# One-hot a step sooner in two buffers, gated outputs split on ScalarE and VectorE: the expert loop of a Flamingo-style two-layer kernel

## Chip, cores and metric

The kernel runs on one core of a Trainium2 chip (trn2). The metric is the device time of one execution in microseconds (us), the median of several. TensorE (PE) multiplies, ScalarE (ACT) and VectorE (DVE) work element by element, GpSimd (POOL) too, SyncE (SP) issues the DMAs. Each engine takes its own instructions in order and waits on semaphores for the others.

## The reference, cut to what matters

There are 128 sequences of 64 tokens, 128 features each. Layer 0 is a gated cross attention and then an expert-choice mixture of experts; layer 1 is a gated cross attention and a routed feed-forward. The change touches the mixture of layer 0 alone, and one shared constant.

```python
gates, idx = jax.lax.top_k(affinity, CAP)            # per sequence and expert: CAP = 32 tokens
expert_in = jnp.take_along_axis(x[:, None, :, :], idx[..., None], axis=2)
h = jax.nn.gelu(jnp.einsum('becd,edf->becf', expert_in, w1) + b1[None, :, None, :])
expert_out = jnp.einsum('becf,efd->becd', h, w2) + b2[None, :, None, :]
out = out.at[jnp.arange(b)[:, None, None], idx].add(gates[..., None] * expert_out)
```

There are 16 experts, and a hidden size of 512.

## The kernel before

`run_experts` works in steps: 8 groups of GB = 16 sequences, 16 experts each, so 128 steps, each one expert on the 16 x 32 = 512 chosen rows of a group. In the text, step j is a body of the loop (`body(a)`, j = a.j, e = a.e counts 1 to 16 in a group). What belongs to one step is spread over several bodies:

- In body j TensorE multiplies first-layer products of step j+1 (12 matmuls of 512 columns into psH, L237), then scatters step j-2 into the token sums psA (16 matmuls of 64 rows, 64 columns of weights and 128 moving columns, L1694), then makes the second-layer products of step j (12 matmuls into psE, L237). Ahead of them stand two matmuls ("takes", L1629) that gather rows for the next group. Values are kept as a high and a low half in fp16, and a product takes three matmuls.
- ScalarE copies half of a take (L1734), applies GELU to psH in four parts (`ft` 0 to 3, L1746), and after parts 1 and 3 makes the high half of h (L1751, 1024 elements a partition). In every second body it makes the high half xn of the next normalised tile, ahead of part 2 (L1741).
- VectorE's order in a body: the other half of the take (L1791), the gated output of step j-1 (psE times the gates, into `grow` or `vals` by parity, L1830), in even bodies the next tile (L1772), at e == 2 the residual of the group before (L1864, reads psA), then the one-hot `put` of step j-2 (L1839), the low half of h (L1820, first part), in even bodies `sel` (L1786), the second low half (L1820), in even bodies the split of the tile (L1777), then some statistics (L186).
- GpSimd casts the gated output to fp16 into eoT (L1613) and makes the low half (L1615).
- SP sends eoT through a transposing DMA to eoZ (L1586), then loads the gates of step j+1 (L1578) and, in every second body, rows for a tile (L1546).

`put` is the stationary operand of the scatter: put[p, k, n] is 1 where slot p of tile k holds token n (N = 64). It has one buffer, [P, GT, N] with GT = 8, so that the next one waits until psA of the step before has been made (`seeded["A"]`, j-3). psE, eoT and eoZ have one buffer each too, and psA has one: at the start of a group the bias matmuls (L1685) wait for the residual. Before psE of step j, TensorE waits until step j-1 has been gated, and before the scatter of step j-2 for `put` and for the transposed eoZ of it.

Three lines outside the loop serve as price rows below: L1061 loads 32 columns of `L` (fp32) with a step of 16 elements (64 bytes), L1445 loads 32 columns of `idx32` (fp32) one behind the other, and L1170 copies 1024 two-byte values a partition on VectorE. L766 is a ScalarE copy from SBUF to SBUF of the size that eoT's high half has.

Of the kernel before, what the change touches and what calls it, by code (L numbers as in the profile page):

```python
# [14 lines left out]
F16 = mybir.dt.float16  # L15
# [6 lines left out]
P = 128  # L22
# [82 lines left out]
def _build(nc, whole, I, out):  # L105
# [37 lines left out]
    ident16 = sb(whole, "ident16", [P, P], F16)  # L143
    ident32 = sb(whole, "ident32", [P, P], F32)
    token_of_p = sb(whole, "token_of_p", [P, 1], F32)
    iota = sb(whole, "iota", [P, P], F16)
    eps_col = sb(whole, "eps_col", [P, 1], F32)
    zero_col = sb(whole, "zero_col", [P, 1], F32)
    gates = sb(whole, "gates", [P, 4], F32)
# [39 lines left out]
    def constants_gpsimd(e, s):  # L189
        e.memset(ident16[:], 0.0).then_inc(s["id"], 1)  # L190
        e.memset(ident32[:], 0.0).then_inc(s["id"], 1)
        e.wait_ge(s["id"], 2)
        for m in (ident32, ident16):
            e.affine_select(out=m[:], in_=m[:], compare_op=ALU.not_equal, fill=1.0, base=0,
                            pattern=[[-1, P]], channel_multiplier=1).then_inc(s["ident"], 1)
        e.iota(token_of_p[:], [[0, 1]], base=0, channel_multiplier=1,
               allow_small_or_imprecise_dtypes=True).then_inc(s["iota"], 1)
        e.iota(iota[:], [[1, P]], base=0, channel_multiplier=0,
               allow_small_or_imprecise_dtypes=True).then_inc(s["iota"], 1)
        e.wait_ge(s["ident"], 2)  # L200
        e.wait_ge(s["iota"], 2)
# [1247 lines left out]
    def run_experts(tag, gate, ew, idx16, vals, tok_slot, rows_odd):  # L1449
# [15 lines left out]
        with ExitStack() as c:  # L1465
            weigh = sb(c, "weigh", [P, GB // 4, P], F16)
            xnf = sb(c, "xnfe", [P, 2, D], F32)
            xn = sb(c, "xne", [P, 2, 2, D], F16)
            pick = sb(c, "pick", [P, 2, P], F16)
            EARLY = GT + 1  # L1470
            first_tiles = first_tiles_in(rows_odd)
            sel = sb(c, "sel", [P, 2, NE * CAP], F16)
# [1 line left out]
                  rows_odd]  # L1474
            g32 = sb(c, "g32", [P, FT, ROWS], F32)
            h = sb(c, "h", [P, 2, 2, FT, ROWS], F16)
            put = sb(c, "put", [P, GT, N], F16)
            lnt = sel[:].rearrange("p a k -> p (a k)").bitcast(F32)[:, 0:4 * NT].rearrange("p (k t) -> p k t", t=NT)

            grow = [sb(c, "grow", [P, GB, CAP], F32), vals]  # L1480
            eoT = sb(c, "eoT", [P, GB, 2, CAP], F16)
            eoZ = sb(c, "eoZ", [P, GT, D], F16)
            psH = ps(c, "psH", [P, 4, 512], F32)
# [55 lines left out]
            with nc.Block() as block:  # L1539
# [63 lines left out]
                    all_steps(e, body)  # L1603
                    e.wait_ge(s["next"], 64)

                @block.gpsimd
                def _(e):
                    for n in range(NE * NG):
                        j = flat(0, 0, n)
                        exact = grow[n % 2][:]  # L1610
                        wait(e, s["gated"], j)
                        wait(e, s["turned"], j - 1, 16)
                        e.tensor_copy(eoT[:, :, 0, :], exact).then_inc(s["eo_hi"], 1)  # L1613
                        wait(e, s["eo_hi"], j)
                        e.tensor_tensor(eoT[:, :, 1, :], exact, eoT[:, :, 0, :], ALU.subtract)\  # L1615
                         .then_inc(s["eo_lo"], 1)

                @block.tensor
                def _(e):
                    def batch_rows(par):  # L1620
# [27 lines left out]
                    def body(a):  # L1648
                        j, par = a.j, a.par
                        tpar = a.k % 2  # L1650
                        if a.has_tile(0):
                            if a.bp == 0:
                                wait(e, s["sel"], a.t)
                                wait(e, late["x_hi"], a.t)
                            else:
                                wait(e, late["x_lo"], a.t)
                                wait(e, s["g_0"], a.t, 2, -1)
                            wait(e, s["gelu"], j, FT)
                            take(tpar, a.bp, (psR[:], psH[:, 3, :]))
                        if a.has(1):  # L1660
                            if a.e % NE == NE - 1:
                                t = a.t - 1
                                wait(e, s["g_0"], t, 2)
                                wait(e, s["g_1"], t, 2)
                            for ft in range(FT):
                                wait(e, s["gelu"], j, FT, ft + 1 - FT)
                                if ft == 3:
                                    if a.has_tile(0):
                                        wait(e, s["g_1"], a.t, 2, a.bp - 1)
                                    else:  # L1670
                                        wait(e, s["g_1"], Step(None, 0, NT - 1), 2)
                                last = matmul3(e, psH[:, ft, :],
                                               [w1[:, hl, a.expert(1), ft * P:ft * P + P] for hl in range(2)],
                                               [a.rows(hl, 1) for hl in range(2)])
                                last.then_inc(s["H"], 1)
                        if a.has(-2):
                            wait(e, s["put"], j - 2)
                            wait(e, s["turned"], j - 2, 16)
                            if a.e == 2:
                                wait(e, seeded["xadd"], flat(a.G, 1, -1))  # L1680
                                wait(e, s["weigh"], flat(a.G, 1, 0), 96)
                                for r in range(RT):
                                    for bp in range(2):
                                        rows = slice(64 * bp, 64 * bp + 3 * NE)
                                        last = e.matmul(psA[:, bp, r, :], weigh[rows, r, :], b2[rows], start=r == 0, stop=False, skip_group_check=True)  # L1685
                                last.then_inc(s["bias"], 1)

                            for r in range(RT):
                                for turn in range(2):
                                    for bp in range(2):  # L1690
                                        side = (bp + turn) % 2
                                        rows = slice(64 * bp, 64 * bp + 64)
                                        to = slice(64 * side, 64 * side + 64)
                                        last = e.matmul(psA[to, bp, r, :], put[rows, RT * side + r, :],  # L1694
                                                        eoZ[rows, RT * side + r, :], start=False,
                                                        stop=a.expert(-2) == NE - 1, skip_group_check=True)
                            last.then_inc(s["A"], 1)
                        if a.has(0):
                            wait(e, s["h_lo"], j, 2)
                            wait(e, s["gated"], j - 1)  # L1700
                            for ft in range(FT):
                                last = matmul3(e, psE[:],
                                               [w2[:, hl, a.expert(0), ft, :] for hl in range(2)],
                                               [h[:, par, hl, ft, :] for hl in range(2)],
                                               ft == 0, ft == FT - 1)
                            last.then_inc(s["E"], 1)
# [3 lines left out]
                def _(e):  # L1710
# [18 lines left out]
                    def body(a):  # L1729
# [6 lines left out]
                        for ft in range(FT):  # L1736
                            if ft == 2 and a.bp == 1 and a.has_tile(1):
                                tpar = (a.k + 1) % 2
                                wait(e, late["ln"], a.t + 1)
                                wait(e, s["g"], a.t - 1, 2)  # L1740
                                e.activation(xn[:, tpar, 0], xnf[:, tpar], ACT.Copy).then_inc(s["x_hi"], 1)  # L1741
                            if a.has(1):
                                wait(e, s["H"], j + 1, FT, ft + 1 - FT)
                                if ft % 2 == 0:
# [18 lines left out]
                def _(e):  # L1763
# [48 lines left out]
                    def body(a):  # L1812
# [20 lines left out]
                            queue_tile(a.t + 1, (a.k + 1) % 2)  # L1833
                        if a.e == 2 and a.G > 0:
                            residual(a.G, -1)
                        if a.has(-2):
                            wait(e, seeded["A"], j - 3)
                            of_step = tok_slot[:, a.expert(-2), a.group(-2) * GT:a.group(-2) * GT + GT]
                            e.tensor_tensor(put[:], iota[:, 0:N].unsqueeze(1).broadcast_to([P, GT, N]),  # L1839
                                            of_step.unsqueeze(2).broadcast_to([P, GT, N]), ALU.is_equal)\  # L1840
                             .then_inc(s["put"], 1)
                        h_low(0)
                        if next_tile:
                            select(a.t + 1, (a.k + 1) % 2, False)
                        h_low(1)
                        if next_tile:
                            split_tile(a.t + 1, (a.k + 1) % 2)
                        if a.G == NG - 1 and 4 <= a.e < 4 + 2 * NORM_STAGES and a.e % 2 == 0:
                            stage = (a.e - 4) // 2
                            queue_norm(e, s, lnt, 0, ready1, stage)  # L1850
# [482 lines left out]
```

## Time and profile before

| | |
|---|---|
| median of 3 runs | 1935.6 us (1933.84 to 1941.17) |
| the profiled execution | 1941.25 us, its span 1939.4 us |
| mean granted TensorE clock | 0.974 of full speed |
| PE, DVE, ACT, POOL busy over the span | 93%, 84%, 77%, 49% |
| the expert loop | from about 484 to 1315 us of the span |

The span runs from the first to the last instruction. A busy PE here is not PE at its peak, since matmuls overlap and their ends are modelled; so the distance from one instruction to the same one a step later says more than busy time. A bracket behind an instruction gives the idle time of its engine just before it and who ended it.

### The profile page before, as it was taken

The page shows a single profiled execution, that of the slowest core. Times are in us where ns is not written, and L with a number is a line of the kernel's source. Part 1 is how long each engine was busy: PE and PEld are TensorE (multiplying, and loading weights), DVE is VectorE, ACT ScalarE, POOL GpSimd, SP SyncE. Part 2 cuts the span into 40 slices and gives each one's busy share as a digit, 9 for nine tenths or more (in the row PEclk, how much of TensorE's full clock was granted, in tenths as well). Part 3 has the DMA queues.
Part 4 walks back from the last instruction along what each step waited for, and adds up shares of the span by engine and source line. Part 5 has one row for each costly group of instructions (what it writes and reads, how often), then busy time and mean ns, then how long its engine had stood idle before and what let it go on. Part 6 is the DMA issues. An engine that isn't in the chain of part 4 may idle for free. (4 is left out here: it accounts for less than half of the span.)

```text
span 1939.4 us, 63284 instructions
## 1 busy us (share of the span) xinstructions
PE 1800.5 (93%) x23899; PEld 1080.2 (56%) x23899; DVE 1622.7 (84%) x3128; ACT 1497.9 (77%) x2645; POOL 948.1 (49%) x1174
## 2 busy tenths in 40 slices
PE   6999998895999999999999999887999999999798
PEld 4777786542443334343433434335777777777577
DVE  5999987597888888888888888667999999988754
ACT  5999996575887878787888888665888888888543
POOL 3888886231333333333343333344666666655565
PEclk8999998997999999999999999998999999999899
DMA  7745445495334434443434533534776666644233
GB/s 175 137 95 100 98 93 111 149 362 169 88 90 95 92 89 96 88 98 88 100 88 98 97 91 91 121 83 97 154 161 154 147 148 155 145 83 68 68 110 120
DMA packets 468694, 227.47 MB, mean 117 GB/s; under 512 B 375950, under 2 KB 435254, under 8 KB 468150
## 3 DMA queue, kind: packets, MB, share of 16 engines
q1 hardware_dynamic: 468054, 225.35, 49.6%
q8 instruction: 93, 1.52, 0.3%
q14 instruction: 67, 0.55, 0.1%
q10 hardware_dynamic: 480, 0.05, 0.0%
HBM read 95.88 MB, written 37.09 MB: 69 GB/s over the span
## 5 line engine op out<-in xcount | busy, mean ns | idle before, releaser
L1820 DVE TENSOR_TENSOR h<-g,h 128x1024 f16<-128x1024 f32 x256 | 384.4, 1501 | 121.3 <-ACT h L1751 116.4
L1746 ACT ACTIVATE g<-psH,eb1T 128x512 f32<-128x512 f32 x512 | 330.6, 681 | 44.7 <-PE psH L237 40.7
L237 PE MATMUL psE<-h,ew 128*128 128x512 f16 x1536 | 360.7, 385 | 0.2 <-DVE grow L1830 0.2
L812 POOL TENSOR_TENSOR Ph<-E,Ph 128x512 f16<-128x512 f32 x192 | 222.2, 1157 | 235.8 <-ACT Ph L766 235.8
L1751 ACT ACTIVATE h<-g 128x1024 f16<-128x1024 f32 x256 | 270.5, 1057 | 8.2
L718 ACT ACTIVATE vB<-psV 128x512 f16<-128x512 f32 x384 | 226.1, 589 | 54.4 <-PE psV L616 52.4
L839 DVE TENSOR_TENSOR vB<-psV,vB 128x512 f16<-128x512 f32 x384 | 248.4, 678 | 1.1 <-ACT vB L718 1.0
L237 PEld LDWEIGHTS psE<-h,ew 128*128 128x128 f16 x1536 | 141.5, 99 | 168.7 <-issue 9.8
L616 PE MATMUL psV<-shared 96*64 96x512 f16 x1536 | 210.2, 380 | 1.5 <-DVE vB L839 1.5
L1613 POOL CAST eoT<-grow 128x512 f16<-128x512 f32 x64 | 58.4, 913 | 311.4 <-DVE grow L1830 246.5
L818 POOL TENSOR_TENSOR E<-E,rden 128x512 f32<-128x512 f32 x192 | 200.0, 1042 | 16.3 <-DVE rden L850 15.4
L237 PE MATMUL psH<-shared,ew 128*128 128x512 f16 x768 | 178.2, 382 | 0.0
L237 PE MATMUL psH<-xg,ew 128*128 128x512 f16 x768 | 176.7, 380 | 0.0
L671 PE MATMUL psY<-vB,PT 128*64 128x128 f16 x4608 | 163.6, 220 | 7.9 <-DMA PT<-Ph 6.8
L858 DVE TENSOR_REDUCE top<-psS 128x8 f32<-128x512 f32 x192 | 131.8, 687 | 39.9 <-PE psS L695 39.0
L1613 POOL CAST eoT<-vals 128x512 f16<-128x512 f32 x64 | 43.9, 687 | 245.5 <-DVE vals L1830 197.3
L671 PEld LDWEIGHTS psY<-vB,PT 128*64 128x64 f16 x4608 | 143.7, 110 | 23.9 <-DMA PT<-Ph 15.6
L756 ACT ACTIVATE E<-E,zero_col 128x512 f32<-128x512 f32 x192 | 137.9, 718 | 17.9 <-DVE E L861 15.1
L861 DVE TENSOR_TENSOR E<-psS,top 128x512 f32<-128x512 f32 x192 | 132.8, 692 | 7.8
L695 PE MATMUL psS<-shared,xTa 128*64 128x256 f32 x1024 | 134.4, 383 | 1.9 <-DVE E L861 1.9
L848 DVE TENSOR_REDUCE den<-E 128x8 f32<-128x512 f32 x192 | 130.2, 678 | 5.3 <-ACT E L756 4.3
L627 PEld LDWEIGHTS psU<-shared 96*64 96x64 f16 x3648 | 113.4, 112 | 15.0
(307 smaller groups left out, 3420.0 us busy)
## 6 DMA issues: line engine op xcount, KB each, us to landing
keys_ahead<-shared SPq DMA_DIRECT2D x52, 512.0 KB, 4.7
shared<-keys_ahead SPq DMA_DIRECT2D x52, 512.0 KB, 3.6
grow<-gate_rows SPq DMA_DIRECT2D x64, 256.0 KB, 3.6
vals<-gate_rows SPq DMA_DIRECT2D x64, 256.0 KB
rawe<-in_L_ffn_w_dram SPq DMA_DIRECT2D x32, 256.0 KB, 3.1
wb<-rw SPq DMA_DIRECT2D x64, 128.0 KB, 2.0
idx<-places SPq DMA_DIRECT2D x110, 64.0 KB, 3.0
out_dram<-x SPq DMA_DIRECT2D x7, 512.0 KB, 3.2
```

The source lines that it names most:

```text
L237: last = e.matmul(to, a, b, start=start and n == 0, stop=stop and n == 2, **flags)
L616: last = e.matmul(a.values(b)[half(hp)], cT[:, a.ring, cl, half(b)], Bw[:, bl, a.g, hp].rearrange("p k d -> p (k d)"), start=n == 0, stop= ...
L671: last = e.matmul(psY[half(b), 0:D], PT[:, a4.par, pl, pair, half(b)], vB[:, a4.par, vl, b, pair, :], start=a4.g == n == pair == 0, stop=a ...
L695: last = e.matmul(psS[half(b), h:h + 4, :], xT[:, a.tp, half(b)], u[:, a.slot, h:h + 4, half(b)], start=True, stop=True)
L718: e.activation(vB[:, a.par, 0, b].rearrange("p k d -> p (k d)"), a.values(b), ACT.Copy).then_inc(s["vh" + name], 1)
L756: e.activation(E[:, a1.four], E[:, a1.four], ACT.Exp, bias=zero_col[:], scale=DH ** -0.5)\
L812: e.tensor_tensor(Ph[:, a2.par, 1].rearrange("p k t -> p (k t)"), E[:, a2.four].rearrange("p h l -> p (h l)"), Ph[:, a2.par, 0].rearrange( ...
L818: e.tensor_tensor(E[:, a1.four], E[:, a1.four], rden[:, a1.par, :].unsqueeze(2).broadcast_to([P, 8, N]), ALU.mult)\
L839: e.tensor_tensor(vB[:, a.par, 1, b].rearrange("p k d -> p (k d)"), a.values(b), vB[:, a.par, 0, b].rearrange("p k d -> p (k d)"), ALU.sub ...
L1746: e.activation(g32[:, ft, :], psH[:, ft, :], ACT.Gelu_apprx_tanh, bias=b1T[:, a.expert(1) * FT + ft:a.expert(1) * FT + ft + 1]).then_inc(s ...
L1751: e.activation(h[:, 1 - par, 0, ft - 1:ft + 1, :], g32[:, ft - 1:ft + 1, :], ACT.Copy).then_inc(s["h_hi"], 1)
L1820: e.tensor_tensor(h[:, 1 - par, 1, 2 * q:2 * q + 2, :], g32[:, 2 * q:2 * q + 2, :], h[:, 1 - par, 0, 2 * q:2 * q + 2, :], ALU.subtract)\
```

## The change

`put` gets two buffers and another order of its elements, [P, 2, N, GT]: tokens outermost, the 8 tiles innermost. It is made one body sooner (for step j-1 in body j) and at another place: behind the second low half of h and the tile's split, ahead of the statistics. The constant `iota` grows to [P, N, 8], each token number eight times, so that each operand of the compare is read along its innermost dimension in steps of one element. The scatter's stationary operand is then read with a step of 8 elements (16 bytes). GpSimd has no work in the loop any more: ScalarE makes the high half of the gated output, ahead of GELU part 2, VectorE the low half between the two low halves of h. `pick`, used at the start, lies in the first bytes of `grow[0]`.

```diff
-    iota = sb(whole, "iota", [P, P], F16)
+    iota = sb(whole, "iota", [P, N, 8], F16)
...
-            put = sb(c, "put", [P, GT, N], F16)
+            put = sb(c, "put", [P, 2, N, GT], F16)
...
+            pick = grow[0][:].rearrange("p b c -> p (b c)").bitcast(F16)[:, 0:2 * P].rearrange("p (k t) -> p k t", k=2)
...
-                @block.gpsimd
-                def _(e):
-                    for n in range(NE * NG):
-                        j = flat(0, 0, n)
-                        exact = grow[n % 2][:]
-                        wait(e, s["gated"], j)
-                        wait(e, s["turned"], j - 1, 16)
-                        e.tensor_copy(eoT[:, :, 0, :], exact).then_inc(s["eo_hi"], 1)
-                        wait(e, s["eo_hi"], j)
-                        e.tensor_tensor(eoT[:, :, 1, :], exact, eoT[:, :, 0, :], ALU.subtract)\
-                         .then_inc(s["eo_lo"], 1)
...
-                                        last = e.matmul(psA[to, bp, r, :], put[rows, RT * side + r, :],
+                                        last = e.matmul(psA[to, bp, r, :], put[rows, par, :, RT * side + r],
...
+                            if ft == 2 and a.has(-1):
+                                wait(e, s["gated"], j - 1)
+                                wait(e, s["turned"], j - 2, 16)
+                                e.activation(eoT[:, :, 0, :], grow[1 - par][:], ACT.Copy).then_inc(s["eo_hi"], 1)
...
-                        if a.has(-2):
-                            wait(e, seeded["A"], j - 3)
-                            of_step = tok_slot[:, a.expert(-2), a.group(-2) * GT:a.group(-2) * GT + GT]
-                            e.tensor_tensor(put[:], iota[:, 0:N].unsqueeze(1).broadcast_to([P, GT, N]),
-                                            of_step.unsqueeze(2).broadcast_to([P, GT, N]), ALU.is_equal)\
-                             .then_inc(s["put"], 1)
                         h_low(0)
+                        if a.has(-1):
+                            wait(e, s["eo_hi"], j - 1)
+                            e.tensor_tensor(eoT[:, :, 1, :], grow[1 - par][:], eoT[:, :, 0, :], ALU.subtract)\
+                             .then_inc(s["eo_lo"], 1)
                         if next_tile:
                             select(a.t + 1, (a.k + 1) % 2, False)
                         h_low(1)
                         if next_tile:
                             split_tile(a.t + 1, (a.k + 1) % 2)
+                        if a.has(-1):
+                            wait(e, seeded["A"], j - 3)
+                            of_step = tok_slot[:, a.expert(-1), a.group(-1) * GT:a.group(-1) * GT + GT]
+                            e.tensor_tensor(put[:, 1 - par], iota[:], of_step.unsqueeze(1).broadcast_to([P, N, GT]),
+                                            ALU.is_equal).then_inc(s["put"], 1)
```

## Rows read from the trace of the kernel before

**Rows 1.** Waits in 500 to 1310 us: waiter, releaser: total us, times, longest.

```profile
PE psA L1694 <- DVE put L1839: 27.8, 51, 3.0
PE psA L1685 <- DVE put L1839: 11.2, 7, 1.7
PE psA L1694 <- DMA eoZ<-eoT: 5.7, 8, 4.1
```

**Rows 2.** Busy time by engine in the loop's stretch.

```profile
493.76:1315.00 821.24, 769.62 (x5342) 322.81 (x5340) 681.69 (x867) 653.33 (x916) 281.54 (x254) 0.99 0.42 94
```

**Rows 3.** Timeline of an odd and an even body: start, length, engine, line, idle before.

```profile
839.73 0.42 PE L1694 MATMUL psA<-eoZ,put 64*64 64x128 f16 x16
...
843.10 2.76 PE L237 MATMUL psH<-xg,ew 128*128 128x512 f16 x12
843.21 0.60 ACT L1734 ACTIVATE shared<-psH 128x512 f16<-128x512 f32 x1 [0.65 <-PE psH L1629]
...
843.96 1.33 ACT L1746 ACTIVATE g<-psH,eb1T 128x512 f32<-128x512 f32 x2 [0.15 <-PE psH L237]
...
846.34 0.42 PE L1694 MATMUL psA<-eoZ,put 64*64 64x128 f16 x16 [0.48 <-DVE put L1839]
846.41 1.97 DVE L1820 TENSOR_TENSOR h<-g,h 128x1024 f16<-128x1024 f32 x1
...
846.69 2.76 PE L237 MATMUL psE<-h,ew 128*128 128x512 f16 x12
...
847.77 1.06 ACT L1751 ACTIVATE h<-g 128x1024 f16<-128x1024 f32 x1
...
848.86 1.23 DVE L1820 TENSOR_TENSOR h<-g,h 128x1024 f16<-128x1024 f32 x1 [0.20 <-ACT h L1751]
...
849.71 2.76 PE L237 MATMUL psH<-xg,ew 128*128 128x512 f16 x12
849.82 0.60 ACT L1734 ACTIVATE shared<-psH 128x512 f16<-128x512 f32 x1 [1.00 <-PE psH L1629]
850.00 0.28 DVE L1777 TENSOR_TENSOR xne<-xnfe,xne 128x128 f16<-128x128 f32 x1
850.20 0.29 DVE L186 BATCH_NORM_STATS2 stats<-x 128x6 f32<-128x128 f32 x1
850.40 0.68 DVE L1791 CAST shared<-psR 128x512 f16<-128x512 f32 x1
...
851.00 0.68 DVE L1830 TENSOR_TENSOR grow<-psE,grow 128x512 f32<-128x512 f32 x1
851.59 0.68 DVE L1839 TENSOR_TENSOR put<-iota,tok_slot 128x512 f16<-128x512 f16 x1
...
852.41 0.42 PE L1694 MATMUL psA<-eoZ,put 64*64 64x128 f16 x16
...
```

**Rows 4.** Timeline at the start of a group, body e == 2.

```profile
908.56 1.41 DVE L1864 SCALAR_TENSOR_TENSOR x<-psA,tanh_g,x 128x512 f32<-128x512 f32 x2
...
909.88 1.02 DVE L1839 TENSOR_TENSOR put<-iota,tok_slot 128x512 f16<-128x512 f16 x1
...
910.95 0.40 PE L1685 MATMUL psA<-eb,weigh 48*128 48x128 f16 x8 [1.72 <-DVE put L1839]
```

**Rows 5.** Costliest lines by form: busy us, mean ns.

```profile
L766 ACT ACTIVATE Ph<-E 128x512 f16<-128x512 f32 x192 | 119.1, 621 | 0.6 <-POOL E L818 0.6
L1170 DVE COPY xg<-psXs 128x1024 f16<-128x1024 f16 x16 | 11.0, 687 | 17.3 <-PE psXs L1072 17.3
```

**Rows 6.** Weight loads of three lines, from each line's own view: min/median/max ns.

```profile
L1061 PEld LDWEIGHTS psZ<-ident,L x128: 127/134/149, 357.9 to 374.4; 64*32 64x32 f32 x128
...
L1445 PEld LDWEIGHTS psI<-ident,idx x128: 106/109/171, 443.5 to 456.0; 128*32 128x32 f32 x128
...
L1694 PEld LDWEIGHTS psA<-eoZ,put x2048: 102/107/174, 497.0 to 1313.0; 64*64 64x64 f16 x187
```

**Rows 7.** The view of tile eoZ: its DMA from issue to landing.

```profile
DMA to landing us min/median/max: 3.0/3.1/9.1
```

More of the change, by code:

```diff
@@ L197, in constants_gpsimd @@
                allow_small_or_imprecise_dtypes=True).then_inc(s["iota"], 1)
-        e.iota(iota[:], [[1, P]], base=0, channel_multiplier=0,
+        e.iota(iota[:], [[1, N], [0, 8]], base=0, channel_multiplier=0,
                allow_small_or_imprecise_dtypes=True).then_inc(s["iota"], 1)
@@ L1468, in run_experts @@
             xn = sb(c, "xne", [P, 2, 2, D], F16)
-            pick = sb(c, "pick", [P, 2, P], F16)
             EARLY = GT + 1
```

## Prediction

> **What bounds the kernel now.** I read the page first, for the loop's place, then the busy times of its stretch, the list of waits, the timeline of two bodies, the timeline at a group's start, and last the lines whose shapes price what is new. In the loop TensorE shows 770 of 821 us busy and nearly the full clock (0.99), VectorE 682, ScalarE 653, GpSimd 282 [rows 2]. So TensorE sets the pace where it can, and the question is what it waits for. The list of waits answers: the scatter's matmuls stood 27.8 us, 51 times, until `put` was made, the bias matmuls at a group's start 11.2 us, 7 times, and only 5.7 us were owed to the transposed eoZ [rows 1].
>
> The timeline shows where. From one scatter to the next it is 846.34 - 839.73 = 6.61 us, then 852.41 - 846.34 = 6.07 [rows 3]. The second is TensorE's own work without a gap: 12 matmuls, scatter, 12 matmuls, takes. The first has 0.48 us of idle before the scatter, and is 0.55 longer, as every even body is: there the tile's instruction stands ahead of `put` on VectorE. The reader is to see two more things. ScalarE stands idle before its half of the take, 0.65 us in one body and 1.00 (plus what TensorE was late) in the other [rows 3]: that is its slack. And VectorE's second low half of 1024 elements takes 1.23 us in its quiet moments, but the first 1.97, while GpSimd works too [rows 3].
>
> **Edit 1, `put` a step sooner, in two buffers.** It takes the wait for `put` away in all but the group's first scatter. The waits are 27.8 us of idle, and since 0.48 us of idle stood for 0.55 us of a step, I count 27.8 x 0.55 / 0.48 = 32 us. The new `put` comes at the end of body j for body j+1's scatter, some 1.5 us before it is due (851.1 against 852.4 in the walk below, less what TensorE is held), so nothing of that wait should be left.
>
> **Edit 2, its price on VectorE.** `put` now costs 0.68 us for 512 elements [rows 3]. L1170 moves 1024 two-byte elements in 687 ns [rows 5], the same time for twice the elements, and the new order gives the compare operands that also run in steps of one. From 512 to 1024 fp32 elements VectorE's time grows from 0.68 to 1.23 us [rows 3], so 256 cycles less are about 0.27: I take 0.41 us. The bounds are 0.41 and 0.68.
>
> By the Trainium skill, VectorE: DVE Perf Modes, the perf-mode tier table, a `tensor_tensor` on 16-bit SBUF operands runs at two elements a cycle when all step by one; no such instruction is in this trace, and the row nearest to it, L1170, agrees in rate.
>
> **Edit 3, the strided weights.** Stationary columns now lie 16 bytes apart. The nearest rows: a load of 32 fp32 columns takes 109 ns in sequence and 134 ns with a step of 64 bytes [rows 6], 25 ns more, 0.8 ns a column. A scatter load has 64 columns, so 50 ns more on its 107. The 16 matmuls of 216 ns take 0.42 us together [rows 3, 6], which means four rounds of four quadrants, each round (0.42 - 0.216) / 3 = 0.07 us behind the one before. If the four loads of a round still run side by side, each round is 0.05 longer: 4 x 0.05 = 0.20 us a step, on the path, because TensorE has nothing between. The low end is 0 (two-byte elements and 16 bytes may be read for nothing; L1061 has 64). The high end is that left and right loads, which read the same partitions, take turns: a round is then 2 x (0.07 + 0.05) = 0.24 against 0.07, or 0.67 us a step. I take 0.20, since L1061 is the only strided load there is, and it did pay. Over 127 scatters: 0, +25 or +85 us.
>
> The Trainium skill, SBUF — State Buffer, section on Door 1 (the note on cachelines), speaks against this change: lines are 16 bytes, an operand needs two hits in a line for the full rate, and each access that crosses to a new line pays. L1061 agrees that crossing costs; the page gives no price, and in the same note it calls a step of 8 two-byte elements free, by which the sum would have 0 here.
>
> **Edit 4, eoT on ScalarE and VectorE.** A ScalarE copy of this shape lasts 621 ns [rows 5]; consecutive instructions overlap by 0.08 (VectorE's do: 850.00 + 0.28 against 850.20 [rows 3]), so 0.53 us more in each body, behind the first high half of h. The slack of 0.65 and 1.00 covers it, so ScalarE delays no take; without the slack it would be 0.53 a step. The second high half, and the low half that waits for it, come 0.53 later. VectorE pays 0.68 more for eoT's low half, the time of L1830 in the same size, and gets back what GpSimd cost it (1.97 - 1.23 = 0.74 in that one instruction [rows 3]). It lies between the two low halves, where VectorE would wait for ScalarE.
>
> What is late next is the gating, on which psE waits. Walk the end of an even body: second high half done at 847.77 + 1.06 + 0.53 = 849.36; low half to 850.60; split to 850.80; `put` to 851.13; statistics to 851.34; take copy to 851.94; gating to 852.54. Without any stall, psE would be due 6.06 after 846.69 - 0.55, at 852.20 [rows 3]. So gating is 0.35 late in even bodies, some 50 times: 17 us, if weights cost nothing. With 0.20 in each of the two scatters that lie between (0.40), psE is due at 852.60 and nothing is late. The two costs exclude each other for the most part. In odd bodies there is no tile, split or statistics, and gating is in time.
>
> **The transposes.** They are issued when VectorE's low half of eoT is done: psH's start + 0.86 + 1.33 (two GELUs) + 1.06 (high half) + 1.23 + 0.68, about 5.2 after it, and land 3.1 later [rows 7] at 8.3, while the next scatter is due at 2.69 + 6.06 = 8.75 (the unstalled scatter comes 846.34 - 0.55 - 843.10 = 2.69 after psH's start [rows 3]). Slack 0.45, less than now. Most land in 3.1; a few are slow, and each will cost more: +1.5 us in all.
>
> **The group's start.** There the residual (1.41 us) and `put` (1.02) stand ahead of the bias matmuls, which wait 1.72 [rows 4]. The residual stays, `put` goes, but the body begins about 0.85 later (0.53 from ScalarE, 0.33 for the new `put` of the body before). Residual done at 908.56 + 1.41 + 0.85 = 910.82, against 910.95 now: 0.1 gained, and the stride of one scatter hides in the stall. 7 x 0.3 = 2 us. The stall of 11 us stays: the change does not reach it.
>
> **Sum.** -32 + 25 - 2 + 1.5 = -7.5 us, in the profiled execution 1941.3 (span 1939.4) to about 1934. That execution lies 5.6 above the median, so for the median 1935.6 - 7.5 = 1928, and I say 1928.
>
> **Rivals.**
>
> *Strided loads are free* (0.22). Then -32 + 17 - 1 + 1.5 = -15: 1921; if the late gating does not show either, 1904. For it: the step is only 16 bytes. Against it: L1061.
>
> *Strided loads are dear, so the kernel is slower* (0.20). Left and right loads share what reads a partition. It decides from the price at which 127 p outweighs 32 + 2: p = 0.27 us a scatter. At 0.40: +51 - 33 = +18, 1953. At 0.67: +85 - 37 = +48, 1984. For it: two loads on the same rows now read 128 columns in a round of 0.07 us; against it: nothing in the trace shows two strided loads on the same rows, either way.
>
> *`put` still runs at one element a cycle* (0.08), the repeated operand being the reason. Its 0.27 more make gating late by 0.35 + 0.27 - 0.40 = 0.22, 50 times 11 us: +4, 1940. So the compare's new order would not do what it is laid out for, and the buffers alone would carry the rest.
>
> *ScalarE becomes the bound* (0.08). Odd slack is 0.65 - 0.53 = 0.12. If the copy waits for the gating, as it may in odd bodies, or takes 0.15 longer than 0.53 and nothing else moves, each step pays about 0.1: +13 on the sum, 1941. A longer scatter gives it room again, which is why I rate it low.
>
> The forecast itself has 0.42, and its own range is 1922 to 1937.
>
> **Range and chances.** A measurement tells 0.5%, 9.7 us: faster is under 1925.9, slower over 1945.3. Faster: the free case, 0.22, and a third of the forecast's, 0.14: 0.36. Slower: the dear case 0.20, and 0.04 from the last two: 0.24. The rest, 0.40, is no difference. The range runs from 1915 (the free case with half of the late gating) to 1962 (half way into the dear case); it leaves out some 0.05 below and 0.12 above.
>
> **What would show it.** Right: GpSimd without work in the loop; no wait of L1694 for `put`; steps of equal length in odd and even bodies, near 6.26 us; the scatter's 16 matmuls in about 0.6 us instead of 0.42, loads of 157 ns instead of 107; `put` at 0.41 us; VectorE's L1820 at 1.23 on the mean; the bias matmuls still 1.6 us late. Wrong: scatter loads at 107 and psE waiting for the gating (free case), a scatter of 0.8 us or more (dear case), idle time of TensorE that ends on a ScalarE instruction (ScalarE as the bound), or long waits for eoZ, which would mean that the later issue of the transposes was the step that I priced too low.

## The result and the profile after

| | median us | lowest to highest | executions |
|---|---|---|---|
| before | 1938.72 | 1933.84 to 1941.17 | 6 |
| after | 1952.41 | 1945.84 to 1956.97 | 6 |

The ratio is 1.0068, 95% interval 1.0053 to 1.0083: the changed kernel is slower by 13.7 us, where 7.5 us of gain were forecast. Its profiled execution took 1952.59 us, its span is 1950.7.

First the busy time by engine of the changed kernel in the stretch of its loop (start:end, length, then PE, PEld, DVE, ACT, POOL, the granted clock, DMA share, GB/s), which answers to [rows 2]:

```profile
485.00:1318.00 833.00, 807.72 (x5348) 363.37 (x5347) 636.25 (x999) 727.78 (x1055) 0.00 (x0) 0.99 0.43 92
```

GpSimd has nothing left to do, as the change says. ScalarE has 74 us more than before, VectorE 45 less although it does more: its low halves of h last 1225 ns on the mean where they lasted 1509 beside GpSimd, and the compare 418 where it lasted 824. TensorE is busy 38 us longer with the same matmuls. That is where the time is, and it is no wait.

The waits of the changed kernel, 500 to 1320 us (waiter, releaser: total us, times, longest), beside [rows 1]:

```profile
PE psA L1682 <- DMA eoZ<-eoT: 14.2, 12, 6.0
...
PE psA L1673 <- DVE x L1859: 10.3, 7, 1.6
...
PEld psA L1682 <- DVE put L1841: 2.7, 1, 2.7
...
PE psE L237 <- DVE grow L1822: 0.4, 1, 0.4
```

L1682 is the scatter, once L1694; L1673 the bias matmuls, once L1685. The 51 waits of the scatter's matmuls for `put` are gone; one weight load, ahead of the third last scatter (1315.85), still shows one, and eoZ outlasts it there. The bias matmuls still wait 7 times, now for the residual. The waits for the transposed eoZ have grown: ahead of the last group from 0.2 us, once, to 6.0 us in ten, and over the whole loop from 10.7 to 18.9 (the 5.7 of [rows 1] stop short of the last scatter). psE hardly ever waits for the gating.

The scatter from the view of its own line (min/median/max ns), and then from the costliest lines by form what two VectorE lines cost (busy us, mean ns, idle before), beside [rows 6]:

```profile
L1682 PEld LDWEIGHTS psA<-eoZ,put x2048: 188/212/215, 498.7 to 1327.0; 64*64 64x64 f16 x187
L1682 PE MATMUL psA<-eoZ,put x2048: 277/280/377, 498.7 to 1327.0; 64*64 64x128 f16 x187
```

```profile
L1812 DVE TENSOR_TENSOR h<-g,h 128x1024 f16<-128x1024 f32 x248 | 303.7, 1225 | 179.3 <-ACT h L1743 179.2
...
L1841 DVE TENSOR_TENSOR put<-iota,tok_slot 128x512 f16<-128x512 f16 x124 | 51.8, 418 | 0.0
```

A load of the same 64 columns went from 107 ns to 212 (mean 207), the compare to 418 ns. The timeline of the changed kernel shows what that makes of two bodies (start, length, idle before in brackets), beside [rows 3]:

```profile
840.62 0.69 PE L1682 MATMUL psA<-eoZ,put 64*64 64x128 f16 x16
...
841.25 2.76 PE L237 MATMUL psE<-h,ew 128*128 128x512 f16 x12
841.31 0.61 ACT L1733 ACTIVATE eoT<-vals 128x512 f16<-128x512 f32 x1
...
842.38 0.68 DVE L1831 TENSOR_TENSOR eoT<-vals,eoT 128x512 f16<-128x512 f32 x1
...
843.10 1.25 SPq L1586 DMA_TRANSPOSE eoZ<-eoT  x1
...
844.20 1.23 DVE L1812 TENSOR_TENSOR h<-g,h 128x1024 f16<-128x1024 f32 x1 [0.87 <-ACT h L1743]
...
844.38 0.60 ACT L1722 ACTIVATE shared<-psH 128x512 f16<-128x512 f32 x1 [0.21 <-PE psH L1617]
...
845.54 0.42 DVE L1841 TENSOR_TENSOR put<-iota,tok_slot 128x512 f16<-128x512 f16 x1
...
846.20 4.18 SPq L1554 DMA_DIRECT2D weigh<-shares x6
...
846.67 0.68 DVE L1822 TENSOR_TENSOR grow<-psE,grow 128x512 f32<-128x512 f32 x1
...
846.96 0.69 PE L1682 MATMUL psA<-eoZ,put 64*64 64x128 f16 x16
...
847.59 2.76 PE L237 MATMUL psE<-h,ew 128*128 128x512 f16 x12
...
848.73 0.69 DVE L1831 TENSOR_TENSOR eoT<-grow,eoT 128x512 f16<-128x512 f32 x1
...
850.48 1.25 SPq L1586 DMA_TRANSPOSE eoZ<-eoT  x1
...
850.72 0.60 ACT L1722 ACTIVATE shared<-psH 128x512 f16<-128x512 f32 x1 [0.41 <-PE psH L1617]
...
853.68 0.69 PE L1682 MATMUL psA<-eoZ,put 64*64 64x128 f16 x16 [0.31 <-DMA eoZ<-eoT]
```

From scatter to scatter it is 846.96 - 840.62 = 6.34 us, where it was 6.61 and 6.07. TensorE has no gap in it: the 16 matmuls span 0.69 us, not 0.42. The next step is 6.72 long, for another reason: eoT was complete at 849.42, but SP's queue was busy with the loads of `weigh` to 850.38, so that the transpose went out at 850.48 and its eoZ came 0.31 us late for the scatter.

**The ledger.** I took the distances between the first matmuls of successive psE in both traces, 127 each. They add up to 817.1 us before and 830.3 after, 13.1 more (the spans differ by 11.3; a little comes back elsewhere). Four lines explain it:

- the strided loads: a step without any wait goes from 6.06 to 6.34; 127 x 0.28 = +35.6 us
- the waits for `put`: before, 48 of the steps outside the groups' starts exceed 6.06, by 26.5 us together; none does for that reason after: -26.5
- eoZ too late: after, 11 of those steps exceed 6.34 (the longest is 7.50), by 6.9 us together: +6.9
- the rest, the groups' starts and the last group: -2.9

35.6 - 26.5 + 6.9 - 2.9 = 13.1. The last group itself is 2.5 us longer, with one wait of 5.97 for eoZ where it was 4.05. Both traces also have two steps right behind a group's start that are 1.69 us longer than their neighbours (7.75 before, 8.03 after): there the granted clock fell to half, 1.2 GHz, for 3.4 us (from 703.9 and 912.2 before, from 709.2 and 815.0 after), behind the stall of that start; behind the other starts with the same stall it did not. They cancel here, but of the kernels below some have one or three and most have none.

### The profile page after: what moved, and what is told of

Same layout as the page of the kernel before. It is cut to its first block and busy times, and to the rows that moved or that the text cites. A ratio compares the mean times of both kernels' runs of the same rounds, so it can differ in the third digit from the quotient of the medians.

```text
span 1950.7 us, 63284 instructions
## 1 busy us (share of the span) xinstructions
PE 1831.8 (94%) x23899; PEld 1117.5 (57%) x23899; DVE 1573.7 (81%) x3256; ACT 1564.6 (80%) x2773; POOL 663.2 (34%) x918
## 5 line engine op out<-in xcount | busy, mean ns | idle before, releaser
L1812 DVE TENSOR_TENSOR h<-g,h 128x1024 f16<-128x1024 f32 x256 | 313.5, 1225 | 188.9 <-ACT h L1743 188.8
L237 PEld LDWEIGHTS psH<-xg,ew 128*128 128x128 f16 x768 | 71.3, 98 | 90.6 <-issue 11.6
L237 PEld LDWEIGHTS psH<-shared,ew 128*128 128x128 f16 x768 | 70.2, 98 | 91.2 <-issue 16.3
```

Source lines behind the costliest of these rows:

```text
L237: last = e.matmul(to, a, b, start=start and n == 0, stop=stop and n == 2, **flags)
L1812: e.tensor_tensor(h[:, 1 - par, 1, 2 * q:2 * q + 2, :], g32[:, 2 * q:2 * q + 2, :], h[:, 1 - par, 0, 2 * q:2 * q + 2, :], ALU.subtract)\
```

## The experiments

Ratios are to the kernel before on the same chip, with 95% intervals. "Before" had medians of 1939.11, 1939.77 and 1939.79 us in the three batches. A "step" is the distance from one scatter to the next in a stretch with no other wait. Line numbers shift a little between the kernels: the scatter is L1682 or L1694.

**First batch: the stride of the weights.** Two kernels change only how `put` lies in the changed kernel, one gives it back its old order, and one gives the new order to the kernel before and changes nothing else.

a_contig: the changed kernel with `put` in its old order, so that the columns of a load are neighbours and the compare has a repeated innermost operand again:

```
-            put = sb(c, "put", [P, 2, N, GT], F16)
+            put = sb(c, "put", [P, 2, GT, N], F16)
...
-   e.matmul(psA[to, bp, r, :], put[rows, par, :, RT * side + r],
+   e.matmul(psA[to, bp, r, :], put[rows, par, RT * side + r, :],
```

> The changed kernel with put laid out as before (columns of a load in sequence), still in two buffers and a step sooner, the compare then at one element a cycle. Theory (the strided loads took the gain): scatter loads back to 107 ns, the scatter's 16 matmuls to 0.42 us, no wait for put; odd steps 6.06 us. By the walk of the prediction the gating is then late in even bodies by 0.35 + 0.27 us, so an even step of about 6.65, a pair of 12.7, and a time near that of the kernel before (1.000, within 0.3%). Rival 1 (the gating is not late in fact): both steps 6.06, some 30 us faster than before, 0.984. Rival 2 (the stride is not what lengthened the steps): steps stay at 6.34, 1.007.

Measured: 1956.56 us, 1.0085 (1.0065 to 1.0105). Loads are back at 106 ns and the scatter at 0.42 us, the compare at 685 ns, and the time is no better; it is above the 1.000 that was expected. The wait has moved. From its timeline and its list of waits, 500 to 1310 us:

```profile
848.13 0.42 PE L1682 MATMUL psA<-eoZ,put 64*64 64x128 f16 x16
848.39 0.68 DVE L1822 TENSOR_TENSOR grow<-psE,grow 128x512 f32<-128x512 f32 x1
...
849.21 2.75 PE L237 MATMUL psE<-h,ew 128*128 128x512 f16 x12 [0.67 <-DVE grow L1822]
```

```profile
PE psE L237 <- DVE grow L1822: 25.2, 43, 0.7
...
PE psA L1682 <- DMA eoZ<-eoT: 15.0, 13, 6.2
```

psE now waits for VectorE's gating of the step before, since its buffer is still being read: 43 times, up to 0.67 us. Steps are 6.05 and 6.80 in turn, a pair of 12.85 where 12.7 was expected.

b_layout_alone: the kernel before, with the new order of `put` and of the compare's operands, one buffer, same place:

```
-            put = sb(c, "put", [P, GT, N], F16)
+            put = sb(c, "put", [P, N, GT], F16)
```

> The kernel before with the new order of put's elements alone: one buffer, made at the old place, GpSimd still makes eoT. Theory: loads of 207 ns, a scatter of 0.69 us, odd steps 6.34; the compare falls from 0.68 (1.10 beside GpSimd) to about 0.42 to 0.6, which takes most of the 0.55 wait of the even step away: pair about 12.7, time as before (1.000 to 1.004). Rival (the stride costs only in the company of the other edits): loads of 107 ns and a pair near 12.2, 0.985.

Measured: 1938.77 us, 0.9998 (0.9984 to 1.0013). Three scatters of its timeline:

```profile
857.37 0.69 PE L1694 MATMUL psA<-eoZ,put 64*64 64x128 f16 x16
...
863.71 0.70 PE L1694 MATMUL psA<-eoZ,put 64*64 64x128 f16 x16
...
870.05 0.69 PE L1694 MATMUL psA<-eoZ,put 64*64 64x128 f16 x16
```

Every step is 6.34. Before, they were 6.06 and 6.61 in turn, 6.34 on the mean. The waits for `put` fell from 27.8 to 4.2 us. The wider scatter leaves VectorE 0.28 us more in each step, and the compare fell from 824 to 561 ns on the mean; how much each of the two did was not taken apart. The wait of 0.55 in every second step became 0.28 in each: the stride costs as much as the wait did, with one buffer still.

c_step4 and d_step2: the changed kernel with `put` cut into blocks of 4 or of 2 tiles, so that the columns (tokens) of a load lie 8 or 4 bytes apart, while the compare still finds runs of 4 or 2 in steps of one. Shown is the kernel with 4 bytes:

```
-            put = sb(c, "put", [P, 2, N, GT], F16)
+            put = sb(c, "put", [P, 2, 4, N, 2], F16)
...
-   e.matmul(psA[to, bp, r, :], put[rows, par, :, RT * side + r],
+   e.matmul(psA[to, bp, r, :],
+            put[rows, par, (RT * side + r) // 2, :, (RT * side + r) % 2],
```

> The changed kernel with put as [2 blocks][64 tokens][4 tiles]: a load's columns lie 8 bytes apart, the compare still runs along steps of one. Theory A (what costs is that each element lies in another 16 bytes): two elements share 16 bytes, loads near 107 ns, scatter 0.42 to 0.5 us, gating late by 0.35 in even bodies, pair about 12.5, 10 us under before (0.994). Theory B (any step other than one costs the same): loads 207 ns, steps 6.34, time as the changed kernel (1.007). Theory C (price in proportion to the step): loads about 150 ns, steps about 6.2, 1.000.

> As c_step4 with put as [4 blocks][64 tokens][2 tiles]: columns 4 bytes apart, the compare in runs of two. Theory A: loads 107 ns, as c_step4, 0.994. Theory B: loads 207 ns, 1.007. Theory C: loads about 120 ns, 0.996. If the compare no longer runs at two elements a cycle in runs of two, put takes 0.68 instead of 0.42 us and the gating is 0.27 later, pair up to 12.7.

Measured: 8 bytes 1936.87 us, 0.9987 (0.9972 to 1.0002); 4 bytes 1935.67 us, 0.9978 (0.9965 to 0.9990). The scatter's loads, first with 8 and then with 4 bytes:

```profile
L1682 PEld LDWEIGHTS psA<-eoZ,put x2048: 130/142/175, 500.0 to 1313.5; 64*64 64x64 f16 x187
```

```profile
L1682 PEld LDWEIGHTS psA<-eoZ,put x2048: 102/107/175, 498.8 to 1310.1; 64*64 64x64 f16 x187
```

None of the three theories holds at both steps: at 8 bytes the load is near theory C's 150, at 4 bytes at theory A's 107. At 4 bytes the load costs what it costs side by side, and the compare keeps its 419 ns. Against the changed kernel that is 17 us, half of the 35.6 that the stride costs in the ledger. Waits took most of the other half, which the list and a stretch of the timeline of the 4-byte kernel show:

```profile
PE psA L1682 <- DMA eoZ<-eoT: 21.6, 18, 5.9
...
PE psE L237 <- DVE grow L1822: 13.8, 39, 0.7
```

```profile
876.77 0.42 PE L1682 MATMUL psA<-eoZ,put 64*64 64x128 f16 x16
...
877.59 2.75 PE L237 MATMUL psE<-h,ew 128*128 128x512 f16 x12 [0.40 <-DVE grow L1822]
```

**Second batch: VectorE's order.** VectorE idles in each body before its second low half, because ScalarE's high half isn't there yet (0.87 us at 844.20 in the timeline above). The compare stands behind that low half, right ahead of the gating that is late. e_gap takes the 4-byte kernel and puts the compare into the idle time:

```
                         select(...)
+                        (the compare into put[:, 1 - par])
                         h_low(1)
                         split_tile(...)
-                        (the compare into put[:, 1 - par])
```

> d_step2 with the compare moved ahead of the second low half of h, where VectorE stood idle 0.87 to 1.16 us until ScalarE had made the high half. Theory (with cheap loads the kernel is held by the gating, late behind everything that VectorE does after ScalarE's second high half): 0.34 us less stands there, so the even step falls from 6.53 to about 6.15 and the time by some 50 x 0.35 = 17 us against d_step2: 0.989 of the kernel before. Rival (ScalarE's extra 0.53 us or the late transposes hold it, not VectorE's order): even steps stay near 6.5, 0.998.

Measured: 1921.74 us, 0.9914 (0.9897 to 0.9931), 14 us less than the 4-byte kernel. Its timeline:

```profile
857.67 0.42 PE L1682 MATMUL psA<-eoZ,put 64*64 64x128 f16 x16
...
860.04 0.42 DVE L1838 TENSOR_TENSOR put<-iota,tok_slot 128x512 f16<-128x512 f16 x1
861.06 1.22 DVE L1812 TENSOR_TENSOR h<-g,h 128x1024 f16<-128x1024 f32 x1 [0.60 <-ACT h L1743]
...
863.85 0.42 PE L1682 MATMUL psA<-eoZ,put 64*64 64x128 f16 x16
```

The compare is free there: VectorE still idles 0.60 us behind it. Waits for the gating fell from 13.8 to 0.5 us, and the long steps from 6.53 to about 6.19. So the late gating of the prediction is real, and is a matter of order.

f_gap_lofirst and g_after_lofirst ask whether the late transposes can be had earlier by putting VectorE's low half of eoT ahead of its first low half of h; f does it in e_gap, g in the changed kernel itself:

```
-                        h_low(0)
                         if a.has(-1): ... (low half of eoT)
+                        h_low(0)
```

> e_gap with VectorE's low half of eoT ahead of the first low half of h. Theory (the late issue of the transposes costs where a landing is slow): they are issued some 0.6 us sooner, waits of the scatter for eoZ fall from about 20 us to 10, some 5 to 10 us under e_gap if VectorE still reaches the second low half in time. Rival (VectorE now waits for ScalarE there and comes late to the second low half in even bodies): no gain or up to 10 us more than e_gap.

> The changed kernel, its 16-byte step kept, with only VectorE's low half of eoT ahead of the first low half of h. Theory: the steady step stays 6.34, since strided loads set it; the single longer steps (0.4 to 1.2 us over 6.34, some ten of them) shrink by up to 0.6 each, 4 to 7 us less than the changed kernel: 1.003 to 1.005. Rival (those long steps have another cause): unchanged, 1.007.

Measured: f 1930.48 us, 0.9955 (0.9938 to 0.9971), 9 us more than e_gap; g 1953.18 us, 1.0078 (1.0061 to 1.0095), about the changed kernel's own. In g the list of waits reads:

```profile
DVE eoT L1830 <- ACT eoT L1733: 147.5, 120, 6.4
...
PEld psR L1617 <- DVE sel L1778: 27.9, 48, 0.6
...
PE psA L1682 <- DMA eoZ<-eoT: 4.8, 4, 3.9
```

From 500 to 1310 us the waits for eoZ fell from 12.0 to 4.8 us, ahead of the last group from 6.0 to 0.9: they do come from the late issue, since the scatter now comes 4.48 us behind it on the median where it was 3.87. A part of these 0.6 us is the longer step. But VectorE then stands before ScalarE's copy, `sel` comes late, and every second step is 6.51 instead of 6.34. The one gain pays for the other loss, so the 4 to 7 us that were expected did not come.

**Parts alone.** h_put_alone is the kernel before with only the early, doubled `put` (4-byte step, compare in the idle time); GpSimd keeps eoT. i_old_layout_gpsimd is the same with the old order and the old, slow compare; l_step8_gpsimd the same with the 16-byte step of the change.

```
-            put = sb(c, "put", [P, GT, N], F16)
+            put = sb(c, "put", [P, 2, 4, N, 2], F16)   (i: [P, 2, GT, N], l: [P, 2, N, GT])
...
-                        if a.has(-2): ... e.tensor_tensor(put[:], ...)
...
                         select(...)
+                        if a.has(-1): ... e.tensor_tensor(put[:, 1 - par], ...)
                         h_low(1)
```

> The kernel before with the early, doubled put alone (made in VectorE's gap, step of 4 bytes), GpSimd still making eoT. Theory (moving eoT to ScalarE and VectorE was what made the gating and the transposes late): without it neither is late, odd and even steps 6.06 to 6.1, 32 us gone as first counted: 0.985. Rival (VectorE beside GpSimd is too slow, its 1.97 us low half and long compares make the gating late too): even steps 6.2 to 6.4, 0.990 to 0.996.

> h_put_alone with put in the old order of elements: the early, doubled compare in VectorE's gap at one element a cycle. Theory (the place in the gap hides the compare, whichever its rate): 0.27 us more in a gap that GpSimd's company has already narrowed, even steps up to 0.2 longer, 0.989 to 0.993. Rival (the compare's rate is needed): even steps 6.5 and more, 0.998 or over.

> h_put_alone with the 16-byte step of the change, GpSimd still making eoT. Theory (the strided loads alone set the steady step of the changed kernel): every step 6.34, scatter 0.69; against h_put_alone 0.28 x 110 = 31 us more, less what hides in stalls, so 1.001 to 1.004 of the kernel before. Rival (the move of eoT is what sets it): steps near 6.1, 0.990.

Measured: h 1917.49 us, 0.9885 (0.9866 to 0.9905); i 1922.17 us, 0.9913 (0.9894 to 0.9933); l 1934.37 us, 0.9974 (0.9963 to 0.9984). In h the steps are 6.06 to 6.10 but for a few longer ones, in l 6.34. So the early `put` in the idle time is worth 22 us, the 16-byte step takes back 17 of them, and the compare's speed matters little there: in i it lasts 1052 ns on the mean, beside GpSimd, in h 757. For l some 31 us over h were expected. The loop of h has 22 waits of the scatter for eoZ, 22.3 us, that of l 4, 10.6 us, all in the last group, so a part of what the stride costs was waiting in h.

h and e_gap have the same `put` in the same place and differ only in who makes eoT: GpSimd in h, ScalarE and VectorE in e_gap. They are 1917.49 and 1921.74 us, so with the compare in the idle time the move of eoT costs 4 us.

j_eot_alone is the other part: the kernel before with only eoT moved from GpSimd to ScalarE and VectorE.

```
-                @block.gpsimd ... e.tensor_copy(eoT[:, :, 0, :], exact) ...
...
+                            if ft == 2 and a.has(-1): ...
+                                e.activation(eoT[:, :, 0, :], grow[1 - par][:], ACT.Copy)
...
+                        if a.has(-1): ...
+                            e.tensor_tensor(eoT[:, :, 1, :], grow[1 - par][:], eoT[:, :, 0, :], ALU.subtract)
```

> The kernel before with eoT moved to ScalarE and VectorE, and nothing else: put as before, one buffer, at its old place. Theory (the move costs): the wait for put stays and grows, since the body begins some 0.5 us later on VectorE while put itself falls from 1.10 to 0.68 without GpSimd: even steps 6.6 to 6.8, odd ones 6.06 to 6.3, 1.000 to 1.010. Rival (freeing VectorE of GpSimd's company is worth more than the 0.68 added): 0.993.

Measured: 1954.99 us, 1.0079 (1.0065 to 1.0094): 15 us slower by itself. Its list of waits, to be read against [rows 1]:

```profile
PE psA L1682 <- DVE put L1831: 44.4, 67, 1.0
```

VectorE's low half of h fell from 1509 ns to 1223 on the mean and `put` from 824 to 681, but 0.68 us of eoT's low half came in and ScalarE's high halves later, so `put` is later than before: 67 waits instead of 51, 44.4 us instead of 27.8.

k_residual is h_put_alone with the residual one body sooner, the wait that the prediction said the change doesn't reach:

```
-                        if a.e == 2 and a.G > 0:
-                            residual(a.G, -1)
                         h_low(0)
+                        if a.e == 1 and a.G > 0:
+                            residual(a.G, -1)
```

> h_put_alone with the residual a body sooner, behind the first low half of h of e == 1: the group's start then has no residual ahead of the bias matmuls. Theory: the step of 7.5 to 7.6 at a group's start falls to 6.4 (the bias matmuls' own 0.33 stays), with 0.3 to 0.6 given back in e == 1 where the residual fills more than the gap: 4 to 7 us under h_put_alone, 0.985. Rival (VectorE's lateness in e == 1 makes the gating late by as much): as h_put_alone, 0.9885.

Measured: 1909.71 us, 0.9852 (0.9832 to 0.9872), the fastest kernel here. The bias matmuls of h_put_alone, then those of this kernel, at the start of the same group:

```profile
697.02 0.40 PE L1685 MATMUL psA<-eb,weigh 48*128 48x128 f16 x8 [1.17 <-DVE x L1863]
```

```profile
693.43 0.40 PE L1685 MATMUL psA<-eb,weigh 48*128 48x128 f16 x8
```

The wait is gone: six group starts of 7.45 to 7.63 us became 6.39 to 6.56, and that of the last group went from 6.61 to 6.21, 7.3 us together. The medians are 8 us apart.

## Why the prediction was wrong

The mechanisms were those of the prediction; three of its terms had the wrong size, and all three errors went the same way. The largest, and the only one that by itself turns the forecast gain into a loss, is the price of the strided weights. In its own order:

**Edit 1, `put` in two buffers.** The waits went, as said. The size was 5.5 us too large. I turned 27.8 us of idle into 32 by the ratio of one step; the steps themselves exceed 6.06 by 26.5 us. The 27.8 hold the longest wait of [rows 1], 2.98 us at 1301.32 near the loop's end, which the second buffer can't take away: the eoZ of that scatter landed only at 1301.03, and in the changed kernel a scatter near the end waits 2.25 us, at 1315.88, for eoZ. `put` is ready 1.0 us ahead of its scatter (845.96 against 846.96), where I had put 1.5; it was enough.

**Edit 2, the compare.** Taken as 0.41 us, measured 0.418. The repeated operand did not hinder it, so the rival that it would stay at 0.68 falls. That it was worth much falls too: with the old compare in VectorE's idle time (i against h) the loss is 4.7 us. It costs in its late place, where it delays the gating: there it is 20.9 us (a_contig against d_step2, both with loads of 106 or 107 ns), some 3 of which are steps at half the clock, three against one.

**Edit 3, the strided weights: the step that failed.** I took 0.8 ns a column from L1061 [rows 6] and so 157 ns a load and 0.20 us a scatter. It is 207 ns, 1.6 ns a column, and 0.69 - 0.42 = 0.27 us a scatter, 0.28 a step: 35.6 us instead of 25.4. A second error hid a part of the first. I let a round grow by as much as its load; with the load's 0.10 us that would be 0.40 a scatter, and 0.27 came. L1061 has fp32 elements and half the columns; it was the only row, but it said nothing of two-byte elements, and 0.8 was no bound. The prediction's own turning point for "slower" was 0.27 us a scatter, so this term alone uses up the gain. The loads of a round do run side by side (in the changed kernel's trace the four start within 0.01 us of one another), and the extreme of 0.67 did not come. The rival of dear loads named 1953 us, and 1952.4 was measured, but that is luck: its 1953 stood for 0.40 us a scatter, by loads that take turns. The stated range holds the measured time only because it reaches into that case. The Trainium skill, SBUF — State Buffer, section on Door 1, calls a step of 8 two-byte elements free in its note on cachelines; the loads of the changed kernel disagree, and the measurement decides. The same note's other sentence, that an operand needs two hits in a 16-byte line, fits the runs at 16 bytes (one hit, 207 ns) and at 4 (four hits, 107), but not at 8, where two hits cost 142.

**Edit 4, eoT on two engines.** ScalarE's copy took 0.61 us and fitted into the slack, of which 0.21 and 0.41 us are left; no take is late, and ScalarE is not the bound. L1812 came to 1.225 us on the mean, as said. The walk to the gating was right too, and so was the remark that the two costs exclude each other: with the stride psE waits 0.4 us in all, without it 0.40 us at a time, 39 times, where I had put 0.35 in some 50. Missing in the prediction is the balance of this edit by itself. I booked it as free but for the gating and 1.5 us of transposes; alone it costs 15 us while `put` is late, and 4 us where `put` is early and the compare stands in the idle time.

**The transposes.** Put at +1.5 us, measured +6.9 in 11 steps ahead of the last group (the ten waits, and one of 0.09 us that the list leaves out); in that group the longest wait for eoZ is 1.9 us longer (5.97 against 4.05). The median landing is 3.1 us as before. Two of the 11 steps follow a transpose that stood behind the `weigh` loads in SP's queue, 1.07 and 1.41 us long, as the one at 850.48 above; I had counted no queue. The other nine were issued at once (0.03 us after eoT) and landed slowly, after 3.9 to 4.9 us: the scatter came 4.0 to 5.0 us after the issue. Slow landings are nothing new. Ahead of the last group the kernel before has seven of 3.9 to 4.8 us, and of its scatters one waited for eoZ, 0.2 us, for from issue to scatter it had 5.07 us on the median; the changed kernel has 3.87. That is 0.8 over the median landing, more than my 0.45, and still too little for every tenth or so. l_step8_gpsimd, where GpSimd hands eoT over earlier, has 5.29 us, slow landings up to 4.9, and no wait for eoZ ahead of the last group. Here is one of the nine, from the timeline of the changed kernel, issued at 656.71 and due at 661.48 - 0.83 = 660.65:

```profile
656.71 1.24 SPq L1586 DMA_TRANSPOSE eoZ<-eoT  x1
...
661.42 0.63 ACT L1733 ACTIVATE eoT<-grow 128x512 f16<-128x512 f32 x1 [0.26 <-DMA eoZ<-eoT]
...
661.48 0.70 PE L1682 MATMUL psA<-eoZ,put 64*64 64x128 f16 x16 [0.83 <-DMA eoZ<-eoT]
```

So it is the later issue that turns slow landings into waits. Why some land slowly was not settled, and a second buffer for eoT and eoZ was not tried.

**The group's start.** Right: the stall stays, 10.3 us in 7 waits against 11.2, now with the residual as its releaser. A start is 8.30 us against 8.18.

**The sum.** -32 + 25 - 2 + 1.5 = -7.5 against +13.1 in the ledger: 20.6 apart. The stride accounts for 35.6 - 25.4 = 10.2, the waits for `put` for 32 - 26.5 = 5.5, the transposes for 6.9 - 1.5 = 5.4, together 21.1; the rest is the groups' starts (-2.9 against -2, the last group in it) and the 25.4 that I rounded to 25. With the stride alone at its measured size the sum is about +3; with the other two alone put right it is +3 as well, and with either of them alone still a gain of 2. The forecast held "equal steps near 6.26"; they are equal, at 6.34.

**By parts**, as shares of the kernel before: the early `put` with loads of 107 ns and in the idle time is -1.15%, the new order alone 0.0%, the 16-byte step on top of the early `put` +0.9%, eoT moved alone +0.79%, and on top of the early `put` +0.3%. Between l_step8_gpsimd and the changed kernel, which have the same steady step, lie 18 us in the loop's sum: 5 in six groups' starts (7.45 against 8.30), 6.9 in late transposes, 3 in the last group with its start, and 3.4 in the two steps of 8.03 us in which the granted clock fell to half, of which l has none. They differ in the compare's place as well as in who makes eoT, so these 18 us are not eoT's alone; with the same `put` in the same place it was 4 (e_gap against h_put_alone).

## What to carry to other kernels

- An order of a tensor that speeds its maker may slow its reader: price the layout where it is read, on the engine that bounds the kernel. Here blocks of two served both.
- A faster or relieved engine helps only through the hand-off that is late. Look first for idle time in the in-order engine ahead of the late instruction and move work into it: that was worth 14 us for the compare, and making the residual a body sooner another 8; neither cost a resource.
- When a stall and a new cost exclude each other, take each away by itself before judging either: the stride hid the late gating, and its removal alone gave half of what it cost.
- A DMA's slack is to be held against its slow landings and not its median: 0.8 us over the median of 3.1 were too little here, where 2.0 had been enough.

## What the hardware showed that was not expected

- The price of a stationary operand's column step, for loads of 64 two-byte columns in 64 x 64 tiles: 107 ns at 2 and at 4 bytes, 142 at 8, 207 on the mean at 16. The scatter of 16 matmuls takes 0.42, 0.42, 0.46 and 0.69 us.
- The compare on VectorE keeps its 0.42 us for 512 two-byte elements when the operands run in steps of one over only two elements, with a repeated dimension outside; with the repeat innermost it takes 0.68.
- Beside GpSimd the same instructions can be stretched a good deal: the 0.42 us compare of h_put_alone to 1.38 at most, 0.757 on the mean. It depends on how they meet: in l_step8_gpsimd, with GpSimd doing the same work, the mean is 0.412. And taking GpSimd's work away did not pay: alone it cost 15 us, since 0.68 us of it came onto VectorE, whose `put` TensorE waits for.
- Slow landings of the transposing DMA: 3.1 us on the median, but 3.9 to 4.9 for seven and nine of some 110 ahead of the last group, before and after.
